# Loads of w7 on a queue of their own: who issues a weight stream beside label slabs

## The reference, cut to what matters

```python
q1 = _attn_pool(x, mask, w1, b1, w2)
q2 = _attn_pool(x, mask, w3, b3, w4)
h = jnp.concatenate([q1, q2], axis=1) @ w5 + b5
f6 = h @ w6 + b6
iu, ju = jnp.triu_indices(E, k=1)            # E = 300
g = (v @ v.T)[iu, ju]
cross = h[:, iu] * h[:, ju] * g              # 1024 x 44850
f7 = cross @ w7 + b7                         # w7: 44850 x 300
out8 = jnp.concatenate([f6, f7], axis=1) @ w8 + b8
z = jnp.einsum('bu,bku->bk', out8, label_embedding)   # labels: 1024 x 200 x 300
h = jnp.concatenate([z, dense_ctx], axis=1)
h = jnp.maximum(h @ W_top1 + b_top1, 0.0)
h = jnp.maximum(h @ W_top2 + b_top2, 0.0)
y = h @ W_top3
```

## Time and profile before

| | us |
|---|---|
| median of 3 runs (1904.67 to 1905.32) | 1904.72 |
| the profiled execution, its own time | 1907.12 |
| its span in the trace | 1905.3 |
| TensorE busy | 1705.5 |
| VectorE busy | 1630.6 |
| ScalarE busy | 1077.2 |
| GpSimd busy | 602.6 |
| queue of SyncE's loads, share of the 16 DMA engines' time | 67.6% |
| queue of GpSimd's gathers, same | 10.0% |
| granted clock of TensorE, share of full speed | 0.958 |

### The profile page before, as it was taken

The page is one execution under the profiler, slowest core; times in us unless marked ns, Lnnn a source line. Parts: engine busy times, 40 slices in busy tenths (PEclk is TensorE's granted clock), DMA queues, the critical chain, the costliest instruction groups (busy, mean ns, idle before and its releaser), DMA issues. The chain is left out here.

```text
span 1905.3 us, 26124 instructions
## 1 busy us (share of the span) xinstructions
PE 1705.5 (90%) x7084; PEld 1254.8 (66%) x7084; DVE 1630.6 (86%) x5626; ACT 1077.2 (57%) x3457; POOL 602.6 (32%) x427
## 2 busy tenths in 40 slices
PE   2889799999989999999999999999897999997751
PEld 1656567777766777776777777667675777775531
DVE  5999879989998999996999989887995699467766
ACT  3786584764478444666455864766453454454425
POOL 7776507726420553011332158302010000000053
PEclk8899999999999999999999999999998999999975
DMA  9489945749957699775998488687858799789965
GB/s 273 114 296 317 344 155 193 249 147 335 376 229 287 257 354 413 307 275 216 410 365 307 168 296 318 243 340 284 334 193 362 311 382 421 265 301 419 420 277 241
DMA packets 97054, 561.70 MB, mean 295 GB/s; under 512 B 15567, under 2 KB 15941, under 8 KB 71309
## 3 DMA queue, kind: packets, MB, share of 16 engines
q1 hardware_dynamic: 77629, 498.39, 67.6%
q0 software_dynamic: 19264, 61.64, 10.0%
q10 hardware_dynamic: 16, 0.00, 0.0%
HBM read 559.98 MB, written 0.00 MB: 294 GB/s over the span
## 5 line engine op out<-in xcount | busy, mean ns | idle before, releaser
L1024 PE MATMUL acc<-w_sb,prod 128*128 128x300 f32 (+2 forms) x5648 | 1541.9, 423 | 96.6 <-DMA w_sb<-in_w 57.2
L1024 PEld LDWEIGHTS acc<-w_sb,prod 128*128 128x128 f32 (+2 forms) x5648 | 1047.4, 193 | 451.5 <-DMA w_sb<-in_w 70.3
L1254 ACT ACTIVATE prod<-prod,g_all 128x256 f32<-128x256 f32 (+4 forms) x1615 | 690.1, 470 | 488.1 <-DVE prod L793 486.2
L578 POOL DMA_INDIRECT x<-in_tbl,ids_sb x368 | 450.7, 1225 | 465.4 <-DVE qa L683 361.4
L793 DVE TENSOR_TENSOR prod<-fine,coarse 128x1280 f32<-128x1280 f32 (+4 forms) x325 | 423.0, 1307 | 135.2 <-PE coarse L872 132.1
L641 DVE SCALAR_TENSOR_TENSOR junk<-lab,heads 128x300 bf16<-128x300 f32 x1136 | 449.3, 460 | 56.0 <-DMA lab<-in_labels 55.7
L641 DVE SCALAR_TENSOR_TENSOR junk<-x,heads 128x300 bf16<-128x300 f32 x1088 | 429.5, 461 | 25.2 <-DMA x<-in_tbl,ids_sb 22.8
L590 POOL TENSOR_TENSOR lab<-lab,out 128x2400 f32<-128x2400 f32 x18 | 95.8, 5323 | 800.4 <-ACT out L1122 579.7
L683 DVE SCALAR_TENSOR_TENSOR qa<-x,ex,qa 128x300 f32<-128x300 f32 x612 | 279.1, 527 | 0.0
L1147 ACT ACTIVATE waste<-x 128x300 bf16<-128x300 f32 x368 | 162.0, 441 | 26.9 <-DMA x<-in_tbl,ids_sb 25.3
L1068 ACT ACTIVATE picked<-hh 128x256 f32<-128x256 f32 (+4 forms) x325 | 121.5, 375 | 0.0
(11 more groups left out here) (107 smaller groups left out, 554.7 us busy)
## 6 DMA issues: line engine op xcount, KB each, us to landing
w_sb<-in_w SPq DMA_DIRECT2D x320, 750.0 KB, 7.0
lab<-in_labels SPq DMA_DIRECT2D x152, 1200.0 KB, 8.2
x<-in_labels SPq DMA_DIRECT2D x48, 1200.0 KB, 10.3
x<-in_tbl,ids_sb POOLq DMA_INDIRECT x368, 5.6
w_sb<-in_w SPq DMA_DIRECT2D x5, 450.0 KB, 7.2
prod<-in_v_i SPq DMA_DIRECT2D x1, 710.0 KB, 4.3
prod<-in_v_j SPq DMA_DIRECT2D x1, 710.0 KB, 7.0
w_sb<-in_w SPq DMA_DIRECT2D x1, 703.1 KB
```

What stands on the lines that cost most here:

```text
L578: pool.indirect_dma_start(out=row_of(t, n), out_offset=None, in_=tables[n], in_offset=bass.IndirectOffsetOnAxis(ap=ids_sb[:, t, n:n + 1], ...
L1024: last = pe.matmul(acc[:, t % 3, 0:EMB], prod[0:rows, u % RING, m, t % 2 * P:(t % 2 + 1) * P], w7_sb[0:rows, u % W7_RING, m * EMB:(m + 1) ...
L1254: act.activation(chunk, chunk, ACT.Copy, scale=g_all[0:rows, pair:pair + 1]).then_inc(chunk_ready, 1)
```

## The change

The first 4 loads of w7 stay with SyncE. The other 321 are taken out of SyncE's order and issued by ScalarE: behind the last chunk of unit u (at m = 4, before the copies and sums of that tick) it waits until unit u-2 is used and issues the load for unit u+2. The buffer, the bytes and the semaphore that TensorE waits for stay the same, and so does the order of the slabs among themselves.

```diff
             for kind, n in LOADS:
                 if kind == "w7":
-                    if n >= W7_RING:
-                        sp.wait_ge(unit_used, n - W7_RING + 1)
-                    width = chunks_of(n) * EMB
-                    sp.dma_start(w7_sb[:, n % W7_RING, 0:width], w7[n % UNITS][:, 0:width]
-                                 ).then_inc(w7_loaded[n % W7_RING], 16)
+                    if n < W7_RING:
+                        sp.dma_start(w7_sb[:, n, :], w7[n]).then_inc(w7_loaded[n], 16)
                     continue
...
+            def load_w7(n):
+
+                width = chunks_of(n) * EMB
+                act.wait_ge(unit_used, n - W7_RING + 1)
+                act.dma_start(w7_sb[:, n % W7_RING, 0:width], w7[n % UNITS][:, 0:width]
+                              ).then_inc(w7_loaded[n % W7_RING], 16)
+
...
                     if m == 1 and u + RING < TOTAL:
                         pick_window(u + RING)
+                    if m == FINE - 1 and W7_RING <= u + 2 < TOTAL:
+                        load_w7(u + 2)
                     tick = u * FINE + m
                     for name, of, i in COPIES.get(tick, ()):
```

## The result

The changed kernel takes 1918.64 us (median of 4 runs, 1917.79 to 1921.1), the one before 1904.7: ratio 1.0075, 95% interval 1.0057 to 1.0092. A second set, on another chip, gave 1.0065 (1.0049 to 1.008). The forecast was 1901; the time lies in its range (1884 to 1922) but on the other side of the time before. The profiled execution took 1918.23, its span is 1916.4.

What follows compares the result with a forecast made beforehand. No single engine bounds it: TensorE is 90% busy, VectorE 86%, with waits for w7 and slabs. Terms 8.6 + 6.3 + 2 - 4 - 5 - 2 - 3 = 2.9 us faster than 1904.7: 1901.8, said as 1901; range 1884 to 1922.

Steps and rivals of the forecast that it cites:

- step 4: Slabs VectorE waits for: w7 loads now beside them make each 0.6 to 0.9 us later at seven waits; -5 us.
- second stall: TensorE's 9.89 us w7 wait at 1460.5 behind six slabs: goes, but a later slab limits the gain; +6.3 us.
- step 1: The two long w7 stalls behind slabs, at 234.7 and 1460.5: w7's own queue removes them; +8.6 and +6.3 us.
- first stall: TensorE's 9.31 us w7 wait at 234.7 behind four slabs: shrinks to under 1 us; +8.6 us.
- Step 2: Small w7 waits of the middle, 9.3 us: partly won where TensorE may set the pace; +2 us.
- Step 3: One-tile head, 101 to 251 us: ScalarE issues w7 loads later than SyncE did, making TensorE late; -4 us.
- Step 5: ScalarE's 321 load issues at 0.33 us each, nearly all hidden in its waiting; -2 us.
- Step 6: Last stretch, 1693 to 1830: DMA engines at full rate, no gain; w7 gives way once to slabs; -3 us.
- A: Rival, last stretch: w7 gets more than half the DMA service and overtakes slabs; 1876 us, half of it 1889; chance 0.20.
- B's mild form: Rival: ScalarE issues so late that DMA engines idle at eight units, plus head's far bound; 1918 us; B's chance 0.22.
- C: Rival: nothing moves; VectorE's order sets the pace, each us won is waited for at the next slab; 1905 us; chance 0.15.

Runs made afterwards that it cites:

- the middle alone: Kernel before, with only the w7 loads of units 46 to 239 issued by ScalarE: 1917.9 us, ratio 1.0062.
- units 4 to 45: Kernel before, with only the w7 loads of units 4 to 45 issued by ScalarE: 1902.8 us, ratio 0.9978.
- Units 240 to 283 alone: Kernel before, with only the w7 loads of units 240 to 283 issued by ScalarE: 1905.7 us, ratio 0.9994.
- experiment 4: ScalarE w7 loads at both stalls, new slab order: 1872.7; first stall, old order: 1902.1; changed kernel issuing earlier: 1915.0; one queue, new order, seven loads moved: 1870.9.
- units 284 to 324 alone: Kernel before, with only the w7 loads of units 284 to 324 issued by ScalarE: 1908.1 us, ratio 1.001.
- the four parts of the change: Kernel before, w7 on ScalarE only for units 4 to 45, 46 to 239, 240 to 283 or 284 to 324: 1902.8, 1917.9, 1905.7, 1908.1 us.

## Why the prediction was wrong, step by step

The sum had +2.9 us (plus is faster here); the run gave -13.9. The step that failed first is step 4, "slabs that no longer run alone": -5 was taken, and the middle alone measured -11.8 (the step's bound was -18). The mechanism was named, that w7 loads beside a slab make it late, and priced too low. For each wait I took "a third to a half" of a w7 load's 1.83 us, at perhaps seven waits. That wasn't so far off for the waits that were there: the eight slabs of the table that were waited for before grew by 8.3 us, between -2.7 and 4.0 each. What the step left out is what it had at nothing: four slabs that nobody had waited for (4.5 us), and a follower, GpSimd's slab 101, whose 4.0 us of lateness moved a multiplication onto VectorE's copy, which then took 5.12 us. A w7 load was in flight beside nearly every slab, one being issued each 5.2 us, and the slabs with one beside them came 0 to 2.0 us later; a whole load for each would have been too much.

The second step that failed is the second stall in step 1: +6.3 was taken and +1.1 measured.

- Step 1, first stall (+8.6): right in the trace. The stall shrank to 0.53, w7 landed in 4.1 to 7.4 us, and VectorE's products went from 3.7 behind to 6.7 ahead. In the median units 4 to 45 give 4.2, which includes step 3.
- Step 1, second stall (+6.3 net): the stall went as said, and the slab of 1478.6 was next as said. Its landing was mis-sized: 1489.8 instead of 1477.5 (34 + 2.9 + 2 us from 1437.7 on is in fact 1476.6). I counted the bytes ahead of it at 420 GB/s from the time of the burst, but the burst itself came 8.6 us later than before (1446.31 against 1437.67), VectorE and TensorE being late by then, and w7 went on taking a part of each moment. Units 240 to 283 alone gave +1.1, with an interval that takes in no change.
- Step 2 (+2): the small w7 waits of the middle did shrink, from 9.2 to 2.6 us, and the rest came at 690 to 725 us. A gain from it can't be told apart from step 4's loss.
- Step 3 (-4): in the right place. TensorE waits 6.6 us for w7 in the head, at most 3.0 at a time, and the first trace loses 3.9 us between units 4 and 36, others 8 to 11. A cause that I had not counted is that SyncE, without w7 waits, sends the four slabs into the head 17 to 48 us earlier.
- Step 5 (-2): nothing is seen. The chunks of a unit take as long with a load among them as without (experiment 4).
- Step 6 (-3): the DMA engines are at their full rate as said, 410 GB/s, and the cost is a ramp paid once: 1.9 us for units 284 to 324 alone (its interval just takes in no change), 4 to 7 in the traces.
- The rivals. A (w7 overtakes slabs) is reversed: slabs landed in 9.3 us instead of 13.0 from 1700 to 1820, w7 in 11.9 us as before (12.0), and slabs were used no sooner. B's mild form has the right time, 1918, by luck: it blamed ScalarE's late issue and idle DMA engines. C's picture of each microsecond waited for again at the next slab holds nearly at the second stall (0.7 us are left in the changed kernel's trace).

The Trainium skill, "DMA: Bandwidth & Descriptors", section "Issuing engines are not separate DMA queues", had it that a second issuing engine saves the issue time only. In rate the trace agrees (410 and 420 GB/s). In latency it doesn't: w7's 22.9 us went to 7.4 and slab 105's 5.2 to 7.0. The same page, section "Queues, rings and completion order", says that each DMA engine takes turns between the queues it has work for. By that rule a slab that used to be first in the one line shares with the load beside it, and slab 105's 1.8 us fit that. What a turn is worth isn't shown: turns row by row would give slabs 62% of the bytes, and they had 56% from 1710 to 1740 (7.06 MB against 5.60).

What stays open: how much of the head's loss is late issue and how much early slabs (the medians don't show the 8 to 11 us of the traces); what the held copy weighs in the median; and why the four parts of the change add up to 4 to 6 us less than the whole.

## What to carry to other kernels

A second queue moves waiting from one stream to the other; ask who waits for the stream that used to be first in the line. Here a slab came up to 2.0 us later for one load beside it and 3.9 with more traffic, and a third of the added waiting was for slabs that nobody had waited for. When a load is late behind others in one line, first move it up in that line: seven places changed gave 11 us, where the second queue lost 14. And if an engine stands in front of data that was issued last, let it take data that is already there: eight slabs taken one or two places later gave 22 us, and with it the second queue cost nothing more.

## What was unexpected of the hardware

- VectorE is held by GpSimd in some instructions only. In the kernel before, 176 products with `heads` and 10 with `coarse` (one input in PSUM) lie wholly inside one of GpSimd's 22 multiplications and kept their 0.46 and 1.48 us, while a weighted sum with all operands in SBUF took 4.16 us instead of 0.52, and ended 0.3 us behind the multiplication:

```profile
1386.15 4.16 DVE L683 SCALAR_TENSOR_TENSOR qa<-x,ex,qa 128x300 f32<-128x300 f32 x1
```

```profile
1383.90 6.08 POOL L590 TENSOR_TENSOR lab<-lab,out 128x2400 f32<-128x2400 f32 x1 [74.37 <-DMA lab<-in_labels]
```

  It goes the other way too: the weighted sum before this one began 0.4 us after the multiplication and kept its 0.52 us, and this multiplication took 6.08 us, the others up to 5.31, as if it had waited for the sum. The Trainium skill, "SBUF — State Buffer", section "SBUF: two separate sides", says so: a VectorE instruction in a fast mode or with two SBUF inputs and a GpSimd instruction shut each other out for its whole length. The traces agree, with 0.16 to 0.39 us for the copies beside no multiplication and up to 5.12 for one beside it. The prediction did not count on it; it is also why a maximum in place of the copy, with two inputs in SBUF, was no remedy.
- ScalarE issues a load that stands behind its activations while they still run, 2.4 us ahead of the end of the last (the rows of experiment 4). A wait of the first of them still holds the load back.
- A slab that is first in one queue lands in 5.2 us with a w7 load issued 0.4 us behind it on that queue, and in 7.0 with one issued 0.1 us before it on another (slab 105).
